# Two-column transposes of x, channel-wise split of d, separate buffers for the last image's g2 parts

## The reference, cut to what matters

```
x = x + L0(gn(x));  x = x + L1(gn(x))          # gn: group norm, 32 groups of 4 channels
L0: t1 = einsum('nchw,he->ncew', x, p1)        # h (32) -> e (16)
    t3 = depthwise conv 9x9 of t1;  t4 = conv over 4-channel groups, 5x1
    t5 = einsum('ncew,ewf->ncf', t4, p5);  t6 = 3-tap filter over f
    out = einsum('ncf,nfp->ncp', t6, three row-shifted copies of gn(x)) / sqrt(384)
L1: cH, cV, cD = Haar details of gn(x), each resized to 32x32
    y = conv_w . concat(gn(x), cH, cV, cD);  out = relu(batchnorm(y))
```

## Time and profile before

| | |
|---|---|
| three runs | 304.57, 305.17, 308.76 us; median 305.17 |
| profiled execution | 307.2 us, its span 305.5 us |
| mean granted clock of TensorE | 0.924 of full speed |
| busy over the span | PE 83%, DVE 79%, ACT 65%, POOL 54% |
| stage A, t1 | 0 to 38.6 us |
| stage B, convolutions and mixes | 38.6 to about 83 us |
| stage C, the splits of d | about 83 to 103 us |
| main loop | 103 to about 267 us |
| last image, batch norm's factors | about 267 to 280 us |
| relu, sum, stores | 280 to 305.5 us |

### The profile page before, as it was taken

The page is one execution under the profiler, slowest core; times in us unless marked ns, Lnnn a source line. Parts: engine busy times, 40 slices in busy tenths (PEclk is TensorE's granted clock), DMA queues, the critical chain, the costliest instruction groups (busy, mean ns, idle before and its releaser), DMA issues.

```text
span 305.5 us, 6666 instructions
## 1 busy us (share of the span) xinstructions
PE 254.4 (83%) x2662; PEld 194.9 (64%) x2662; DVE 241.6 (79%) x483; ACT 199.8 (65%) x267; POOL 163.7 (54%) x183
## 2 busy tenths in 40 slices
PE   7899978999694998999999999999999999580000
PEld 4333345665484777888998889988899886450000
DVE  2899996045499567778999989999899997786992
ACT  1778822277487443774788777887778877256990
POOL 4000000987635423677888898888988888600000
PEclk9999999999879599999999999999999999985555
DMA  7996031668601700000000000000000000000798
GB/s 226 409 410 226 0 119 35 179 188 261 175 4 36 277 0 0 2 0 3 0 0 2 1 0 2 1 0 2 0 0 2 2 0 3 0 0 27 315 403 354
DMA packets 11487, 28.00 MB, mean 92 GB/s; under 512 B 2528, under 2 KB 3616, under 8 KB 11456
## 3 DMA queue, kind: packets, MB, share of 16 engines
q1 hardware_dynamic: 8624, 21.37, 19.7%
q10 hardware_dynamic: 1232, 4.46, 3.9%
q0 software_dynamic: 1600, 1.74, 2.3%
HBM read 16.39 MB, written 8.39 MB: 81 GB/s over the span
## 4 chain that ended last, share of the span: by engine, by line
PE 67%; DVE 12%; issue 7%; POOL 4%; DMA 3%; ACT 3%; SPq 0%; DVEq 0%; POOLq 0%
PE low L621 9%; PE low L232 9%; PE high L597 9%; PE low L234 8%; PE low L233 8%; DVE x_sb L1019 5%; PE high L732 4%; PE high L232 4%; PE high L233 4%; PE high L234 4%; DVE d_split L809 4%; PE high L635 3%; DMA x_sb<-in_x 3%; PE high L738 2%; POOL g_lo L402 2%
## 5 line engine op out<-in xcount | busy, mean ns | idle before, releaser
L266 POOL DMA_DIRECT2D d_st<-t_sb x50 | 24.7, 501 | 52.6 <-ACT t_sb L456 52.2
L402 POOL TENSOR_TENSOR g_lo<-y_sb,g_hi 128x1024 fp32r<-128x1024 f32 x15 | 36.2, 2411 | 14.4 <-ACT y_sb L552 14.4
L378 POOL TENSOR_TENSOR g_lo<-y_sb,g_hi 128x1024 fp32r<-128x1024 f32 x15 | 35.8, 2387 | 7.8 <-ACT g_hi L511 7.8
L232 PE MATMUL low<-g_hi,t_hi 128*128 128x512 f32 x96 | 37.6, 392 | 1.3 <-DVE t_lo L910 0.7
L234 PE MATMUL low<-g_hi,t_lo 128*128 128x512 f32 x96 | 37.5, 391 | 0.0
L233 PE MATMUL low<-g_lo,t_hi 128*128 128x512 f32 x96 | 37.4, 389 | 0.0
L550 ACT ACTIVATE g_hi<-x_sb,rs 128x1024 fp32r<-128x1024 f32 x16 | 21.3, 1330 | 21.9 <-POOL rs L387 18.7
L800 DVE STREAM_TRANSPOSE xa<-x_sb 128x1024 f32<-128x1024 f32 x15 | 28.0, 1944 | 6.8 <-DMA x_sb<-in_x 6.8
L597 PE MATMUL high<-xa,p_blk 128*128 128x512 f32 x64 | 29.9, 617 | 1.2 <-DVE xa L800 1.2
L809 DVE TENSOR_TENSOR d_split<-d_st,d_split 128x272 fp32r<-128x272 f32 x20 | 15.0, 813 | 19.7 <-ACT d_split L468 19.7
L621 PE MATMUL low<-t_all,taps 32*32 32x272 f32 (+1 forms) x960 | 24.1, 399 | 7.3 <-issue 6.9
(11 more groups left out here) (146 smaller groups left out, 691.8 us busy)
## 6 DMA issues: line engine op xcount, KB each, us to landing
out<-x_sb SPq DMA_DIRECT2D x6, 1024.0 KB, 4.9
x_sb<-in_x SPq DMA_DIRECT2D x11, 512.0 KB, 10.3
x_sb<-in_x ACTq DMA_DIRECT2D x8, 512.0 KB, 12.0
taps<-in_taps SPq DMA_DIRECT2D x6, 320.0 KB, 3.5
d_st<-t_sb POOLq DMA_DIRECT2D x50, 34.0 KB, 3.1
mix<-in_mix SPq DMA_DIRECT2D x6, 256.0 KB, 7.4
out<-x_sb SPq DMA_DIRECT2D x3, 512.0 KB, 2.8
d_st<-t_sb SPq DMA_DIRECT2D x30, 34.0 KB, 4.0
```

The source lines that it names most:

```text
L232: nc.tensor.matmul(ps, w[0], m[0], start=start, stop=False)
L266: eng.dma_start(d_st[32 * jl:32 * jl + 32, r % DR, co].rearrange("p b k -> p (b k)"), t4_sb[32 * co:32 * co + 32, r % 2, jl].rearrange("p ...
L378: pool.tensor_tensor(g1_lo[:, W:W + HW], y_sb[:, n, :], g1_hi[:, W:W + HW].bitcast(F32), ALU.subtract).then_inc(s["g1_lo"], 1)
L402: pool.tensor_tensor(g2_lo[:, :], y_sb[:, n, :], g2_hi[:, :].bitcast(F32), ALU.subtract).then_inc(s["g2_lo"], 1)
```

## The change

Four edits. (1) Every image is transposed in two halves of 16 rows h; a block of 32 is now 16 rows of two neighbouring columns (8 bytes together, then a stride of 128 bytes). `xa`, its waits and `p1_blk` follow: each matmul takes one half of h, 512 contiguous columns, and waits for its own half. (2) `d_high` and `d_low` iterate with the 4 channels innermost: contiguous in `d_split` (16 bytes), and in the source 1,088 bytes apart (`d_st`) or 272 bytes apart (PSUM). (3) Image 15's g2 parts go to buffers of their own, in the place of p5's hi part; ACT's g2_hi(15) waits for the last t5 in place of y(14). ACT's `y_square(12)` comes after g2_hi(15), DVE's `y_own(13)` after g2_lo(15), and zh's columns of image 15 are POOL's work. (4) The group average of image 15 stands between z(14)'s products with g2_hi and those with g2_lo.

```
+        last_hi = put("last_hi", [HW], F32R)
+        last_lo = put("last_lo", [HW], F32R)
...
-        xa = put("xa", [XR, W, G])
+        xa = put("xa", [XR, 2, J, G])
...
+            return (g2_hi, g2_lo) if n < N - 1 else (last_hi, last_lo)
...
-                v = d_split[:, :, part, :, :].rearrange("p n j (b g c) -> p b g c j n", b=B, g=R)
+                v = d_split[:, :, part, :, :].rearrange("p n j (b g c) -> p b g j n c", b=B, g=R)
...
-                if 2 <= t <= N:
+                if t >= 2:
                     z_columns(t - 2)
...
-                if n >= 1:
+                if n == N - 1:
+                    act.wait_ge(s["t5"], NO)
+                elif n >= 1:
                     act.wait_ge(s["y_mm"], n)
...
-                if t >= 4:
+                if t >= 4 and t != N:
                     y_square(t - 4, 1)
                 if 1 <= t <= N:
                     g2_full_and_high(t - 1)
+                if t == N:
+                    y_square(t - 4, 1)
...
-                for v in range(2):
-                    if i == N and v:
-                        pe.wait_ge(s["xa"], i + 1)
-                    rhs, ps = (xa[:, (i - 1) % XR, v:W:2, :], ps_t1[i % 4]) if i else (ones_row[:, 0:G], ps_t1[0][:, 0:G])
-                    mm = pe.matmul(ps, p1_blk[:, v, :], rhs, start=(v == 0), stop=(v == 1))
+                for hh in range(2):
+                    if i >= 1:
+                        pe.wait_ge(s["xa"], 2 * i - 1 + hh)
+                    rhs, ps = (xa[:, (i - 1) % XR, hh], ps_t1[i % 4]) if i else (ones_row[:, 0:G], ps_t1[0][:, 0:G])
+                    mm = pe.matmul(ps, p1_blk[:, hh, :], rhs, start=(hh == 0), stop=(hh == 1))
...
+                if n == N - 2:
+                    group_average(N - 1)
                 pe.wait_ge(s["g2_lo"], n + 1)
...
-                columns = x_sb[:, n, :].rearrange("p (h w) -> p w h", w=W)
-                if n < N - 1:
-                    dve.transpose(xa[:, n % XR], columns).then_inc(s["xa"], 1)
-                    continue
-                for v in range(2):
-                    dve.transpose(xa[:, n % XR, v:W:2, :], columns[:, v:W:2, :]).then_inc(s["xa"], 1)
+                for hh in range(2):
+                    rows = x_sb[:, n, HALF * hh:HALF * hh + HALF].rearrange("p (k j v) -> p j k v", j=J, v=2)
+                    dve.transpose(xa[:, n % XR, hh], rows).then_inc(s["xa"], 1)
...
-            def z_columns_last():
...
+                dve.wait_ge(s["t5"], NO)
+                dve.tensor_tensor(last_lo[:, :], y_sb[:, N - 1, :], last_hi[:, :].bitcast(F32),
                                   ALU.subtract).then_inc(s["g2_lo"], 1)
...
-                if t == N + 2:
-                    z_columns_last()
+                    y_own(t - 4)
...
-                if y >= 0:
+                if y >= 0 and t != N:
                     y_own(y)
```

More of the change, by code:

```diff
@@ L145, in build @@
         assert cursor[0] <= at_p5
+        cursor[0] = at_hi
+        last_hi = put("last_hi", [HW], F32R)
+        last_lo = put("last_lo", [HW], F32R)
+        assert cursor[0] <= at_hi + 2 * JC * NF * 4
         cursor[0] = region_t - (N - RESIDENT) * HW * 4
@@ L220, in columns_apart, with g2_parts @@
             return v.rearrange("p (r j b) -> p r b j", j=J, b=2)
+        def g2_parts(n):
+            return (g2_hi, g2_lo) if n < N - 1 else (last_hi, last_lo)
         def g1_f(n):
@@ L246, in d_views @@
             if r < RS:
-                form = "p c b (j n) -> p b c j n" if pair else "p c (j n) -> p c j n"
+                form = "p c b (j n) -> p b j n c" if pair else "p c (j n) -> p j n c"
                 src = d_st[:, r % DR, :, some, :].rearrange(form, j=JC)
             else:
-                form = "p b (c j n) -> p b c j n" if pair else "p (c j n) -> p c j n"
+                form = "p b (c j n) -> p b j n c" if pair else "p (c j n) -> p j n c"
                 src = (ps_d if r < R - 1 else ps_t3)[:, some, 0:J * NO].rearrange(form, c=CI, j=JC)
@@ L546, in g2_full_and_high @@
                 norm = dict(bias=rs2[:, n % 2, 4:5], scale=rs2[:, n % 2, 3:4])
-                if n >= 1:
+                if n == N - 1:
+                    act.wait_ge(s["t5"], NO)
+                elif n >= 1:
                     act.wait_ge(s["y_mm"], n)
                 pixels = columns_apart(x_sb[:, n, :])
-                act.activation(rows_of(g2_hi[:, :]), pixels, ACT.Identity, **norm).then_inc(s["g2_hi"], 1)
+                act.activation(rows_of(g2_parts(n)[0][:, :]), pixels, ACT.Identity, **norm).then_inc(s["g2_hi"], 1)
                 if n < N - 1:
@@ L587, in t1_product @@
             def t1_product(i):
-                if i >= 1:
-                    pe.wait_ge(s["xa"], i)
                 if i >= 4:
                     pe.wait_ge(s["t1_hi"], i - 3)
-                for v in range(2):
-                    if i == N and v:
-                        pe.wait_ge(s["xa"], i + 1)
-                    rhs, ps = (xa[:, (i - 1) % XR, v:W:2, :], ps_t1[i % 4]) if i else (ones_row[:, 0:G], ps_t1[0][:, 0:G])
-                    mm = pe.matmul(ps, p1_blk[:, v, :], rhs, start=(v == 0), stop=(v == 1))
+                for hh in range(2):
[3 more added lines that the diff above has]
+                    mm = pe.matmul(ps, p1_blk[:, hh, :], rhs, start=(hh == 0), stop=(hh == 1))
                 mm.then_inc(s["t1_mm"], 1)
@@ L722, in z_product @@
             def z_product(n):
-                pixels = [h[:, :].rearrange("p (i a b j) -> p a b i j", a=2, b=2, i=J) for h in (g2_hi, g2_lo)]
+                pixels = [h[:, :].rearrange("p (i a b j) -> p a b i j", a=2, b=2, i=J) for h in g2_parts(n)]
                 pe.wait_ge(s["g2_hi"], n + 1)
@@ L758, in y_product @@
                         continue
-                    mm = split_product(ps_y[:, q], (w_hi[:, 0, :], w_lo[:, 0, :]), (g2_hi[:, q], g2_lo[:, q]),
+                    mm = split_product(ps_y[:, q], (w_hi[:, 0, :], w_lo[:, 0, :]), [h[:, q] for h in g2_parts(n)],
                                        True, True)
@@ L779, in _ @@
                     z_product(t - 2)
-                if 1 <= t <= N:
+                if 1 <= t < N:
                     group_average(t - 1)
@@ L958, in g2_low_last @@
                 dve.wait_ge(s["g2_hi"], N)
-                dve.tensor_tensor(g2_lo[:, :], y_sb[:, N - 1, :], g2_hi[:, :].bitcast(F32),
+                dve.wait_ge(s["t5"], NO)
+                dve.tensor_tensor(last_lo[:, :], y_sb[:, N - 1, :], last_hi[:, :].bitcast(F32),
                                   ALU.subtract).then_inc(s["g2_lo"], 1)
@@ L1047 @@
     from concourse.bass_utils import run_bass_kernel_spmd
-    p1_blk = np.zeros((B, H, 2, B, 2, E), np.float32)
+    p1_blk = np.zeros((B, H // 2, 2, 2, B, 2, E), np.float32)
     for b in range(B):
         for v in range(2):
-            p1_blk[b, :, v, b, v, :] = L0_conv_p1
+            p1_blk[b, :, v, :, b, v, :] = np.asarray(L0_conv_p1).reshape(2, H // 2, E).transpose(1, 0, 2)
     taps, mix = taps_layout(np.asarray(L0_conv_p3), np.asarray(L0_conv_p4))
```

## The result

Changed kernel: median 302.97 us of 20 runs (lowest 300.51), kernel before: 306.69 us of 20 runs (lowest 304.57). The ratio, changed over before, is 0.9865, 95% interval 0.9833 to 0.9897: about 4 us faster. Both medians come from more runs than the 305.17 us on which the prediction was set. The profiled execution of the changed kernel took 302.3 us, its span 300.6 us (305.5 before).

What follows compares the result with a forecast made beforehand. PE bounds the main loop, so only the transposes, d's split and the end could gain: 3.35 + 1.5 + 0.15 = 5.0 us, from 305.17 to 300.2 us, 1.6% less; range 296.8 to 303.5 us.

Steps and rivals of the forecast that it cites:

- the sum of 5.0 us: Whole kernel: 3.35 us from the transposes, 1.5 from d's split, 0.15 from buffers and average together.
- stage A: Input transposes and t1 matmuls: PE replaces DVE as the limit, matmuls end at 35.2 us in place of 38.57.
- stage C: d's splits up to the clock products and t5: shorter DVE chain, clock products right behind the last mix, 1.5 us less.
- the end: Image 15's last steps: average 0.4 us less, columns on POOL 0.25 more; together 0.15 less, bounds -0.4 and +0.3.
- The lower bound for a half: Half transpose on DVE: 0.61 us, from a sum reading at a step of 8 bytes; upper bound 0.95 us.
- pairs are no faster: Rival, input transposes: column pairs cost 1.90 us per image in place of 1.86, total 304.1 us; chance 0.06.
- 3.35 us less: Input transposes in halves: t1 matmuls end at 35.2 us in place of 38.57, counted fully in the total.
- the 1.5 us of the sum: d's split: clock products before t5 start at 98.27 us, right behind the last mix, in place of 99.76.
- stage C gains more: Rival: PE's unexplained 2.19 us gap before the last mix shrinks, the clock falls later; 298.0 us, chance 0.12.
- the split gives nothing: Rival: d's split with scattered source costs as much as scattered hi and lo did; 301.7 us, chance 0.12.
- the slow one: Rival: d's split doubles from 0.75 to 1.5 us in the chain of 16 `d_low`; 313.7 us, chance 0.05.
- The rival with the clock holding at the end: PE keeps full clock around y(14), clock products and z(15), z(15) starting 1.3 us earlier still; 298.9 us, chance 0.15.

## Why the prediction came out as it did

**Time and sign: right, the size partly by luck.** 300.2 us was set against 305.17, 1.6% less; measured 1.35% (1.0 to 1.7). The median of 302.97 us lies 2.8 us above the forecast, 1.5 of it because the kernel before has a median of 306.69 over 20 runs. Between the two profiled executions the spans differ by 4.9 us, as the sum of 5.0 us has it, but out of other terms: stage A 3.0, stage B -0.8, stage C 2.6, the end 0.15. The mechanism of each edit was right as far as the traces show it; stage B took from the sum, the clock in stage C gave to it, and they partly cancelled.

**Stage A: right.** Predicted 35.2 us and PE as the limit, measured 35.55. The lower bound for a half, 0.61 us, was the right one to take (0.64 measured), and the experiment with single columns gives the upper one's 0.95 as 0.97. So the rival "pairs are no faster" is out: at equal numbers of instructions the rule on lines of the Trainium skill ("Advanced Engine Details and Errata", "Memory Cachelines") and the runs agree, 0.64 us for pairs and 0.97 for single columns.

**What failed: "3.35 us less" was carried through stage B as a plain shift.** The prediction named SP's queue for nothing but x. The third load, however, hangs on t1's end and on DVE's statistics, both of which moved, and it slid beside the first convolution. In the table the first stall is 0.16 to 0.65 us in the four executions where t1 ends late, 1.12 to 1.62 us in the eight with edit 1 and the load in its place, 0.42 us with the load put later and 0.60 us with it left out. B1 is 10.86 us on average in the four and 11.72 in the eight, B 59.37 and 60.73: of 3.0 us about 1.4 are lost. A reader could have found it: the earlier trace rows show when DVE and the transfers end, and every transfer issued behind them had to be placed anew.

What PE waits for there its timeline doesn't name, but the packet records of the fourteen traces do. In the six executions with a first stall of 0.16 to 0.65 us, the first packet of the "instruction" queue behind the first convolution's start starts 0.96 to 1.49 us after it; in the eight with 1.12 to 1.62 us, 1.93 to 2.59 us after it. The stall ends 1.2 to 1.5 us after that packet has landed in all fourteen. It is the same further on: stage B has 106 stalls over 0.4 us in the fourteen traces (the wait for ACT's copy behind the first convolution left out), and 104 of them end 1.05 to 1.75 us behind the landing of such a packet, among them the piece of 1.6 to 2.2 us ahead of the last mix for which the prediction had no releaser. The stalls keep their places in the program: behind 140 and 268 products, behind 991 and 1,119, each pair 128 products or 256 instructions of PE apart. These times say that PE stands at such a place until a piece of its program is there, and that the load made the first piece late: with the load left out it starts at 1.20 us again, though t1 ends at 35.49. That the packets carry PE's program is read from the queue's name, from these times and from these places.

The time didn't come back when the first stall was removed. B is made up of two things that vary from execution to execution. PE's idle pieces in it add up to 9.5 to 13.4 us (10.1 on average in the four executions where t1 ends late, 11.3 in the eight). The rest is 47.5 us in the one execution whose clock stayed full all through B, and 50.8 us in the one that had half clock longest, 10.2 us. Why the later packets and the clock fall differently each time stays open.

**Stage C: mechanism right, term too small.** The clock products start right behind the last mix in all eleven executions with edit 2, the 1.5 us of the sum. Then comes what the sum had at nothing, the clock. In the two profiled executions C is 2.56 us shorter: 1.56 of it is the start of the clock products against the last mix, 0.28 their own length (3.9 us, the last piece at full clock, where it was 4.18), and 0.72 the way from there to t6, where the full clock returns sooner. In seven of the eleven the products ran at full clock from the start, in 2.2 us. C is 9.7 to 11.4 us, on average 10.3, and 12.3 to 14.4, on average 13.6, in the three executions without edit 2. Why the clock had fallen in some executions and not in others (the gap ahead of the last mix was 1.6 to 2.2 us in all) isn't settled. So the rival "stage C gains more" came true in part, by the clock and not by PE's gap, which was 2.19 us before and 1.91 in the changed kernel.

The sizes: four lo parts from SBUF take 2.17 us in a row, 0.54 each (predicted 0.55), four from PSUM 1.47 us, 0.37 each, where I had taken the same 0.55. The twelve of rounds 3, 5 and 4 took 5.6 us in place of 8.4, 2.8 less where 2.4 was predicted. The small operations, costed at 3.9 us as before, took 0.9. Neither mattered, since PE's last mix was the limit. The rival "the split gives nothing" is out, and so is the slow one.

**The end: small, as predicted; that it hit 0.15 us is luck.** Predicted 0.15 us, read 0.15 between the two profiled executions. But E is 17.0 to 17.4 us in the three traces without edits 3 and 4. In the nine that have them and the last clock products it is 15.8 us (two executions), 16.4 to 17.1 (five) or 18.1 to 18.4 (two, whose clock was at half for 6.8 us behind the statistics, against 3.4 in the changed kernel). No difference of 0.15 us can be read from that.

The average ran 0.05 us behind the statistics (0.46 before), z(15) started 7.10 us behind them (7.65 before), and `y_neighbours(15)` 11.57 us (11.73 before): of 0.55 us (predicted 0.4) POOL's columns took back 0.39 (predicted 0.25). g2_hi(15) was ready 3.4 us before PE took it, so the own buffers brought nothing while PE's queue held y(14) and the clock products ahead of z(15); no run has the buffers alone.

The rival with the clock holding at the end did occur, in two of the nine executions that have edits 3 and 4 and the last clock products: there y(14) to z(15) is 3.15 us in place of 4.5 to 6.0, and E 15.79 us, 1.1 us less than in the changed kernel, where the rival said 1.3.

## What to carry to other kernels

When a stage is shortened, list every transfer that is issued behind its end and see what it now lies beside, the "instruction" queue's packets included; a gain upstream pays its way only through all of them. When an edit makes an operand ready earlier, look at what stands before its reader in the reader's own queue: here z(15) moved, by 1.8 us against y(14), only once the clock products ahead of it were taken out. No run takes them out without the own buffers, so how much of that needs the buffers isn't shown. Order an access so that neighbours are read at least two at a time, and price it from the row with the most similar stride.

## What the runs showed of the hardware

- A transpose of 512 elements with single columns 128 bytes apart took 0.97 us back to back, with pairs of columns 0.64.
- DVE's subtraction of 272 elements, mean of one: 0.81 us with two streams scattered in SBUF, 0.61 with the source alone scattered there, 0.43 with the source in PSUM at steps of 272 bytes. ACT's copy of 544: 1.13 us with a scattered source in SBUF, 0.61 with a scattered source in PSUM, 1.23 with the source in PSUM together and only the output scattered in SBUF. ACT's copy of 1,088 neighbouring elements of PSUM took 1.07 us, so at 0.61 for half of that the scattered read of PSUM had little or no price there; for DVE no run has the two side by side.
- Five tiny DVE operations took 0.9 us in the eleven traces where they ran before POOL's subtractions of 384 elements, and 3.9 to 4.0 us in the three where they ran beside them. In each of these three, four of the five ended 0.02 to 0.04 us after one of POOL's subtractions had ended.
- PE's unexplained stalls in the convolutions and mixes ended 1.05 to 1.75 us after a packet of 16,384 bytes of the "instruction" queue had landed, 104 of 106 in fourteen traces. With a load of 0.59 MB beside it, the first such packet behind the first convolution's start came 1.2 us later on average.
